# Softmax sums of queries 256 to 511 taken from exponentials of the first scores, on ScalarE instead of by matmul, in the last fifteen steps of an attention and mixture-of-experts layer

## The chip, the cores and the metric

One core of a Trainium2 chip runs the whole program in one launch. The metric is the device time in microseconds, here a median of three runs.

## The reference, cut to what matters

The layer adds three things: its input x (8 batches x 512 tokens x 512 features), causal attention over the layer norm of x (16 heads of 32), and a top-2-of-8 expert layer over the same norm.

```python
xn = _layernorm(x)
q, k, v = proj(Wq), proj(Wk), proj(Wv)          # 16 heads of 32
q, k = _apply_rope(q, k)
scores = einsum('bhqd,bhkd->bhqk', q, k) / sqrt(32)
scores = where(causal, scores, finfo.min)
attn = softmax(scores)
out = einsum('bhqk,bhkd->bhqd', attn, v) @ Wo.T
x = x + out + experts(xn)
```

The softmax needs, for each query and head, the largest score and the sum of the exponentials. The change concerns that sum.

## The kernel before, in words

The attention is cut into 32 steps n, one for each batch and each group of four heads (HG = 4). Steps 0 to 15 come first, then the experts (71 tiles, lines 801 and 1137), then steps 16 to 31. Every engine has its own program, written out by hand in a fixed order (`step(n)` in the blocks of TensorE, VectorE and ScalarE), and the engines meet at semaphores. No scheduler moves anything: an instruction that waits holds up all that stands behind it on its engine.

The scores are computed twice.

* **First scores** (`scores(m, k)`, line 886), queries on partitions, keys along the row. Their only use is the largest score of each query. Eleven score units k = 0 to 10 (`S_UNITS`, line 245) cover the four heads and the four query blocks i of 128. Units 0 to 2 hold the query blocks 0 and 1 of several heads. Units 3 to 6 are block 2 (384 keys) of heads 0 to 3, units 7 to 10 are block 3 (512 keys). They alternate between two PSUM banks (`BANK_S + k % 2`). VectorE reduces each to its maximum (`largest_score`, line 1322, the instruction on line 1326), and unit k + 2 may be written when unit k is reduced (line 893). Step n does this for step n + 1: it is the look-ahead of one step.
* **Shifted scores** (`shifted_scores(n, k)`, line 906), keys on partitions, queries along the row. The maxima were split into two f16 parts (`split_c`), turned by TensorE (`turn_c`, line 902), copied by ScalarE (`copy_c`, line 705) and sent through DRAM into two more rows of `q_stack`, so that the matmul itself subtracts them. Eleven shifted units go through two banks (`BANK_T`), and ScalarE's `exps(n, k)` (line 696, instruction on line 702) writes their exponentials to `pT`. GpSimd zeroes the masked triangle.

`times_v(n, j)` (line 919) then works on the key block j (0 to 3) of `pT`, queries j x 128 to 511. Four matmuls of 32 output rows, one for each head, add P times V into `BANK_O` (line 928). Four more with a matrix of ones (`ones32`, line 931) add the sums of the exponentials into `BANK_DEN`. All are f32 and run over 512, 384, 256 and 128 columns. Blocks 0 and 1 are done in step n, blocks 2 and 3 in step n + 1. VectorE's `normalise_o(n)` (line 1337) waits for the last of them, turns the sums, takes reciprocals and scales the output; ScalarE's `high_o` (line 711) rounds it for the output projection.

Between these, TensorE's program lays pieces of other work that wait for little: the projections of Q, K and V for later steps (lines 948, 957) and the output projection (line 966). A stretch of TensorE's step reads: shifted unit j, score unit j + 4, three projection matmuls, shifted unit j + 1, score unit j + 5, and so on. VectorE's step does score maxima 0 to 3, `normalise_o(n - 1)`, `rotate(0)` for Q (line 1313), maxima 4 to 8, `rotate(1)`, maxima 9 and 10, `split_c`. Steps 29 to 31 have no projections of Q and K left, steps 28 to 31 none of V, and steps 16 to 27 have all.

## Time and profile before

| | |
|---|---|
| median of three runs | 1181.91 us (1181.77 to 1182.01) |
| the profiled execution's own time | 1190.92 us |
| its span, first to last instruction | 1189.0 us |
| mean granted TensorE clock | 0.916 of full speed |
| TensorE matmuls busy | 984.2 us, 83% of the span |
| VectorE busy | 733.6 us, 62% |
| ScalarE busy | 416.3 us, 35% |
| GpSimd busy | 544.0 us, 46% |
| matmuls with the ones (line 931) | 1024, 94.0 us busy, mean 439 ns |
| P times V (line 928) | 1024, 100.1 us busy, mean 464 ns |
| exponentials (line 702) | 352, 224.1 us busy |
| score maxima (line 1326) | 352, 212.3 us busy |

Busy times count an engine's instructions from start to end, so where matmuls overlap in the array the sum over a group is more than what the group takes of the span. The profiled execution ran 9.0 us longer than the median of the three timed ones, and what the profile shows adds up to its span. Steps 16 to 31 begin at 826.6 us of the span. The program's last score unit stands at 1141.9 us.

### The profile page before, as it was taken

How to read it: one execution, taken by the hardware profiler on the slowest of the kernel's cores; microseconds unless marked ns; L12 is line 12 of the kernel's file. 1: busy time of each engine (PE TensorE's matmuls, PEld its weight loads, DVE VectorE, ACT ScalarE, POOL GpSimd, SP SyncE). 2: the span in 40 equal slices, each digit the busy share in tenths (PEclk: the TensorE clock that was granted, in tenths of full speed). 3: DMA queues.
4: the chain of work that ended last, by engine and by line, in shares of the span. 5: the costliest groups of instructions: out<-in, count | busy, mean ns of one | idle time of the engine just before them, and what ended most of it. 6: DMA issues, size and time to landing. Idle time of an engine off the chain costs nothing.

```text
span 1189.0 us, 18558 instructions
## 1 busy us (share of the span) xinstructions
PE 984.2 (83%) x6525; PEld 460.9 (39%) x6557; DVE 733.6 (62%) x1282; ACT 416.3 (35%) x689; POOL 544.0 (46%) x561
## 2 busy tenths in 40 slices
PE   3659675778769786987859999999999999999886
PEld 1224232333324332432435555554444444444332
DVE  7465665576557665785524444444777777777654
ACT  3243554354444333333311222211443443443441
POOL 1423543353443543457423333331766766765534
PEclk8888787898879887989979999999999999999899
DMA  5446164746655441243565555554546445435224
GB/s 201 120 145 218 44 235 112 229 133 204 205 204 183 155 159 55 73 145 114 205 219 174 175 176 171 177 177 153 179 160 195 147 162 196 143 126 182 83 73 141
DMA packets 107960, 188.60 MB, mean 159 GB/s; under 512 B 11872, under 2 KB 65248, under 8 KB 102624
## 3 DMA queue, kind: packets, MB, share of 16 engines
q1 hardware_dynamic: 97072, 152.03, 37.8%
q0 software_dynamic: 10800, 35.40, 10.2%
q8 instruction: 55, 0.90, 0.3%
q14 instruction: 33, 0.27, 0.1%
HBM read 117.13 MB, written 70.25 MB: 158 GB/s over the span
## 4 chain that ended last, share of the span: by engine, by line
PE 62%; DVE 15%; DMA 9%; issue 5%; ACT 4%; POOL 2%; SPq 2%; POOLq 0%; ACTq 0%; DVEq 0%
PE psum L880 16%; PE psum L948 8%; PE psum L957 7%; PE psum L928 6%; PE psum L897 6%; PE psum L966 5%; PE psum L931 5%; PE psum L915 4%; DVE top L1326 3%; DMA x_blk<-xn_rows 3%; PE psum L857 3%; DMA c_rows<-c_turn 3%; DVE rden L1341 2%; DVE den_turned L1339 2%; DVE turned_q L1319 1%
## 5 line engine op out<-in xcount | busy, mean ns | idle before, releaser
L702 ACT ACTIVATE pT<-psum,factors 128x512 f32<-128x512 f32 (+1 forms) x352 | 224.1, 642 | 466.4 <-PE psum L915 463.4
L897 PE MATMUL psum<-k_stack,q_stack 96*128 96x384 f16 (+3 forms) x512 | 140.4, 328 | 133.0 <-DVE top L1326 123.4
L1326 DVE TENSOR_REDUCE top<-psum 128x1 f32<-128x384 f32 (+3 forms) x352 | 212.3, 634 | 48.3 <-PE psum L899 36.3
L948 PE MATMUL psum<-xT,w_att 128*128 128x512 f16 x768 | 211.6, 404 | 9.4 <-DVE xT L1288 5.3
L880 PE MATMUL psum<-w_exp,x_gT 128*128 x852 | 197.9, 383 | 5.4 <-DVE x_gT L1293 5.4
L915 PE MATMUL psum<-q_stack,k_stack 98*128 98x256 f16 (+3 forms) x512 | 134.9, 316 | 7.1 <-ACT pT L702 6.2
L570 POOL DMA_INDIRECT x_g<-xn_rows,tok_of x71 | 67.3, 947 | 147.6 <-PE psum L857 146.4
L897 PEld LDWEIGHTS psum<-k_stack,q_stack 96*128 96x128 f16 x512 | 48.7, 102 | 198.5 <-DVE top L1326 157.0
L564 POOL TENSOR_TENSOR o_hl<-o_sb,o_hl 128x512 f16<-128x512 f32 x32 | 36.9, 1154 | 189.0 <-ACT o_hl L716 189.0
L558 POOL TENSOR_SCALAR_AFFINE_SELECT pT<-pT 128x512 f32<-128x512 f32 x128 | 86.9, 690 | 77.8 <-ACT pT L702 77.7
L880 PEld LDWEIGHTS psum<-w_exp,x_gT 128*128 128x128 f16 x852 | 83.8, 98 | 92.1 <-issue 8.5
L1307 DVE SCALAR_TENSOR_TENSOR y_sb<-psum,down,bias_all 128x512 f32<-128x512 f32 x71 | 53.3, 751 | 103.7 <-PE psum L880 103.7
L957 PE MATMUL psum<-w_att,xT 128*128 128x512 f16 x384 | 113.0, 426 | 0.0
L948 PEld LDWEIGHTS psum<-xT,w_att 128*128 128x128 f16 x768 | 73.7, 103 | 86.1 <-issue 22.9
L726 ACT ACTIVATE x_gT<-psum 128x512 f16<-128x512 f32 x71 | 42.4, 597 | 182.7 <-PE psum L857 182.7
L966 PE MATMUL psum<-w_att,o_hl 128*128 128x512 f16 x384 | 98.4, 383 | 4.5 <-POOL o_hl L564 4.5
L928 PE MATMUL psum<-pT,v_sb 128*32 128x512 f32 (+3 forms) x1024 | 100.1, 464 | 1.2 <-POOL pT L558 1.2
L931 PE MATMUL psum<-pT,ones 128*32 128x512 f32 (+3 forms) x1024 | 94.0, 439 | 0.0
L899 PE MATMUL psum<-causal,ident 128*128 128x128 bf16 (+1 forms) x320 | 79.2, 248 | 0.0
L915 PEld LDWEIGHTS psum<-q_stack,k_stack 98*128 98x128 f16 x512 | 46.1, 101 | 85.3 <-issue 42.6
L554 POOL TENSOR_TENSOR q_hl<-plain_q,q_hl 128x512 f16<-128x512 f32 x32 | 46.6, 1455 | 61.9 <-ACT q_hl L687 61.9
L580 POOL DMA_INDIRECT y_in<-y_rows,idx_y x64 | 62.6, 979 | 19.7 <-issue 11.1
(153 smaller groups left out, 1240.9 us busy)
## 6 DMA issues: line engine op xcount, KB each, us to landing
y_rows<-y_sb SPq DMA_DIRECT2D x71, 256.0 KB, 2.0
w_in<-w_all SPq DMA_DIRECT2D x12, 1024.0 KB, 8.9
q_stack<-qk_rows SPq DMA_DIRECT2D x96, 128.0 KB, 2.6
k_stack<-qk_rows SPq DMA_DIRECT2D x96, 128.0 KB
x_in<-x SPq DMA_DIRECT2D x8, 1024.0 KB, 9.1
xn_rows<-x_in SPq DMA_DIRECT2D x8, 1024.0 KB, 8.2
qk_rows<-q_hl SPq DMA_DIRECT2D x32, 256.0 KB, 2.1
qk_rows<-k_hl SPq DMA_DIRECT2D x32, 256.0 KB
```

The source lines that it names most:

```text
L558: pool.affine_select(out=p_diagonal(j), in_=p_diagonal(j), compare_op=ALU.is_ge, fill=0.0, base=0, pattern=[[0, HG], [1, P]], channel_mult ...
L702: act.activation(p_of(j, h, heads), banks[BANK_T + (NT_ * n + k) % 2][:, 0:W], ACT.Exp, scale=factors[:, 0:1]).then_inc(exp_done, 1)
L880: now = pe.matmul(banks[s % 4], x_gT[s % 4][:, xp * C + c, :], w_exp[:, bass.ds(e, 1), wp, c, :].rearrange("p e d -> p (e d)"), start=n == ...
L897: pe.matmul(bank[:, h * W:(h + 1) * W], q_stack[u][0:ROW_C, h0 + h, i * P:(i + 1) * P], k_stack[u][0:ROW_C, h0 + h, 0:W], start=h == 0, st ...
L899: pe.matmul(bank[:, 0:heads * W].rearrange("p (h t) -> p h t", h=heads)[:, :, W - P:W], ident16[:], causal[:, 0:heads, :], start=False, st ...
L915: now = pe.matmul(bank[:, h * W:(h + 1) * W], k_stack[u][0:ROW_C + 2, h0 + h, j * P:(j + 1) * P], q_stack[u][0:ROW_C + 2, h0 + h, j * P:S] ...
L928: pe.matmul(banks[BANK_O][h * HD:(h + 1) * HD, j * P:S], v_sb[b % 2][:, j, g * P + h * HD:g * P + (h + 1) * HD], p_of(j, h, 1), start=j == ...
L931: now = pe.matmul(banks[BANK_DEN][h * HD:(h + 1) * HD, j * P:S], ones32[:], p_of(j, h, 1), start=j == 0, stop=j == J - 1)
L948: now = pe.matmul(bank, w_att[:, what, wp, c, g * P:(g + 1) * P], xT[b % 2][:, xp * C + c, :], start=at_pass == 0, stop=at_pass == 3 * C - 1)
L957: now = pe.matmul(banks[bank], xT[b % 2][:, xp * C + c, j * P:(j + 1) * P], w_att[:, 2, wp, c, :], start=at_pass == 0, stop=at_pass == 3 * ...
L966: now = pe.matmul(banks[bank], o_hl[b % 2][:, c, xp, j * P:(j + 1) * P], w_att[:, 3, wp, c, :], start=at_pass == 0, stop=at_pass == 3 * C - 1)
L1326: return dve.tensor_reduce(out=top[:, h:h + heads, i], in_=banks[BANK_S + k % 2][:, 0:heads * W].rearrange("p (h t) -> p h t", h=heads), a ...
```

## The change

For steps n = 17 to 31 (`SUMS` = 17) the sums of query blocks 2 and 3 no longer come from `pT`. In the step before, after the maximum of score units 3 to 10, VectorE multiplies it by minus the scale (`shift_scores`, one number for each partition), and ScalarE takes the exponential of the unit's scores in place in PSUM, with that number as bias, and accumulates it along the row into `den` (`sum_scores`). `times_v` runs its matmuls with ones only over columns 0 to 255, thus for key blocks 0 and 1, and eight new matmuls of 128 columns bring `den` into columns 256 to 511 of `BANK_DEN`: `den`, broadcast over 32 columns, is the stationary operand and the f32 identity the moving one. TensorE's score units 5 to 10, and the next step's unit 0 and `turn_c`, now wait for ScalarE's `den_done`. The rest of the program is the same.

```diff
@@ ScalarE
+            def sum_scores(m, k):
+                h, _, i = S_UNITS[k]
+                here = banks[BANK_S + k % 2][:, 0:(i + 1) * P]
+                act.wait_ge(shift_done, sum_no(m, k))
+                act.activation(here, here, ACT.Exp, scale=factors[:, 1:2], bias=shift_s[:, h, i - J // 2:i - J // 2 + 1],
+                               accum_out=den[:, m % 2, h, i - J // 2:i - J // 2 + 1]).then_inc(den_done, 1)
...
             def step(n):
                 exps(n, 0)
+                if SUMS <= n + 1 < N:
+                    sum_scores(n + 1, 3)
                 exps(n, 1)
+                if SUMS <= n + 1 < N:
+                    sum_scores(n + 1, 4)
                 if n and n != N1:
                     high_o(n - 1)
...
                 exps(n, 2)
+                if SUMS <= n + 1 < N:
+                    sum_scores(n + 1, 5)
                 exps(n, 3)
+                if SUMS <= n + 1 < N:
+                    sum_scores(n + 1, 6)
                 exps(n, 4)
+                if SUMS <= n + 1 < N:
+                    sum_scores(n + 1, 7)
...
                 exps(n, 5)
+                if SUMS <= n + 1 < N:
+                    sum_scores(n + 1, 8)
...
                 exps(n, 6)
+                if SUMS <= n + 1 < N:
+                    sum_scores(n + 1, 9)
                 exps(n, 7)
+                if SUMS <= n + 1 < N:
+                    sum_scores(n + 1, 10)
                 if n + 1 < N:
                     copy_c(n + 1)
@@ TensorE
-                if k >= 2:
+                if k >= 2 and m >= SUMS and k - 2 in SUM_UNITS:
+                    pe.wait_ge(den_done, sum_no(m, k - 2))
+                elif k >= 2:
                     pe.wait_ge(max_done, NS * m + k - 1)
                 elif m:
                     pe.wait_ge(c_copied, m)
+                    if m > SUMS:
+                        pe.wait_ge(den_done, sum_no(m, 0) + SUM_UNITS[0] - 1)
...
             def turn_c(m):
                 pe.wait_ge(c_made, m + 1)
+                if m >= SUMS:
+                    pe.wait_ge(den_done, sum_no(m, NS - 2))
...
-                for h in range(HG):
-                    now = pe.matmul(banks[BANK_DEN][h * HD:(h + 1) * HD, j * P:S], ones32[:], p_of(j, h, 1),
-                                    start=j == 0, stop=j == J - 1)
+
+                upto = S if n < SUMS else S // 2
+                if j * P < upto:
+                    for h in range(HG):
+                        now = pe.matmul(banks[BANK_DEN][h * HD:(h + 1) * HD, j * P:upto], ones32[:], p_of(j, h, 1)[:, 0:upto - j * P],
+                                        start=j == 0, stop=(j + 1) * P == upto)
+                if n >= SUMS and j == 0:
+                    pe.wait_ge(den_done, sum_no(n, NS - 1))
+                    for i in range(J // 2):
+                        for h in range(HG):
+                            now = pe.matmul(banks[BANK_DEN][h * HD:(h + 1) * HD, (J // 2 + i) * P:(J // 2 + i + 1) * P],
+                                            den[:, n % 2, h, i:i + 1].broadcast_to([P, HD]), ident32[:], start=False, stop=False)
                 now.then_inc(pv_done, 1)
@@ VectorE
+                if m >= SUMS and k in SUM_UNITS:
+                    shift_scores(m, k)
+
+
+            def shift_scores(m, k):
+                h, _, i = S_UNITS[k]
+                dve.wait_ge(max_done, NS * m + k + 1)
+                dve.tensor_tensor(shift_s[:, h, i - J // 2:i - J // 2 + 1], top[:, h, i:i + 1], factors[:, 3:4], ALU.mult).then_inc(shift_done, 1)
```

Once, ahead of step 0, two more operations on one number for each partition make the scale and its negative (`factors[:, 1]` and `[:, 3]`).

**ScalarE**, from the rounding of K in one step to the exponentials of the next, one of steps 17 to 28. The names say what is written from what; `pT` are exponentials of shifted units, `o_hl` is `high_o`. Before:

```order
L687 ACTIVATE k_hl<-plain_k 128x512 [waits k_stored,qk_roped]
L702 ACTIVATE pT<-psum,factors 128x512 [waits pv_done,t_done] x4
L716 ACTIVATE o_hl_131<-o_sb 128x512 [waits o_read]
L702 ACTIVATE pT<-psum,factors 128x512 [waits pv_done,t_done] x2
L702 ACTIVATE pT<-psum,factors 128x384 [waits pv_done,t_done]
```

and with the change:

```order
L697 ACTIVATE k_hl<-plain_k 128x512 [waits k_stored,qk_roped]
L712 ACTIVATE pT<-psum,factors 128x512 [waits pv_done,t_done] x3
L719 ACTIVATE psum,den<-psum,shift_s,factors 128x384 [waits shift_done]
L712 ACTIVATE pT<-psum,factors 128x512 [waits pv_done,t_done]
L719 ACTIVATE psum,den<-psum,shift_s,factors 128x384 [waits shift_done]
L733 ACTIVATE o_hl_133<-o_sb 128x512 [waits o_read]
L712 ACTIVATE pT<-psum,factors 128x512 [waits pv_done,t_done]
L719 ACTIVATE psum,den<-psum,shift_s,factors 128x384 [waits shift_done]
L712 ACTIVATE pT<-psum,factors 128x512 [waits pv_done,t_done]
L719 ACTIVATE psum,den<-psum,shift_s,factors 128x384 [waits shift_done]
```

A sum stands behind each exponential of the shifted units 0 to 4 (and behind those of 5 to 7), and `high_o` now has two of them ahead of it.

**TensorE**, the same place in the step, from shifted unit 1 to the projection matmuls behind score unit 6. Before:

```order
L915 MATMUL psum<-q_stack_96,k_stack_99 128x512 [waits exp_done]
L897 MATMUL psum<-k_stack_100,q_stack_97 128x384 [waits max_done]
L899 MATMUL psum<-causal,ident_49 128x128
L948 MATMUL psum<-xT_133,w_att 128x512 [waits sum_done]
L948 MATMUL psum<-xT_133,w_att 128x512 x2
L915 MATMUL psum<-q_stack_96,k_stack_99 128x512 [waits exp_done]
L897 MATMUL psum<-k_stack_100,q_stack_97 128x384 [waits max_done]
L899 MATMUL psum<-causal,ident_49 128x128
L948 MATMUL psum<-xT_133,w_att 128x512 x3
```

and with the change:

```order
L954 MATMUL psum<-q_stack_97,k_stack_100 128x512 [waits exp_done]
L934 MATMUL psum<-k_stack_101,q_stack_98 128x384 [waits den_done]
L936 MATMUL psum<-causal,ident_49 128x128
L996 MATMUL psum<-xT_135,w_att 128x512 [waits sum_done]
L996 MATMUL psum<-xT_135,w_att 128x512 x2
L954 MATMUL psum<-q_stack_97,k_stack_100 128x512 [waits exp_done]
L934 MATMUL psum<-k_stack_101,q_stack_98 128x384 [waits den_done]
L936 MATMUL psum<-causal,ident_49 128x128
L996 MATMUL psum<-xT_135,w_att 128x512 x3
```

No instruction moved, but each score unit from unit 5 on (line 934, before 897) waits for ScalarE's sum of the unit two before it instead of VectorE's maximum.

**VectorE**, from the end of `rotate(0)` to `rotate(1)` and, in the first fence, the two maxima behind it. Before:

```order
L1320 TENSOR_TENSOR plain_q<-psum,trig_sb 128x512
L1326 TENSOR_REDUCE top<-psum 128x1 [waits s_done] x5
L1319 STREAM_SHUFFLE turned_k<-psum 128x512 [waits qk_lo,qk_summed]
L1320 TENSOR_TENSOR plain_k<-psum,trig_sb 128x512
L1326 TENSOR_REDUCE top<-psum 128x1 [waits s_done] x2
```

and with the change:

```order
L1368 TENSOR_TENSOR plain_q<-psum,trig_sb 128x512
L1374 TENSOR_REDUCE top<-psum 128x1 [waits s_done]
L1383 TENSOR_TENSOR shift_s<-top,factors 128x1 [waits max_done]
L1374 TENSOR_REDUCE top<-psum 128x1 [waits s_done]
L1383 TENSOR_TENSOR shift_s<-top,factors 128x1 [waits max_done]
L1374 TENSOR_REDUCE top<-psum 128x1 [waits s_done]
L1383 TENSOR_TENSOR shift_s<-top,factors 128x1 [waits max_done]
L1374 TENSOR_REDUCE top<-psum 128x1 [waits s_done]
L1383 TENSOR_TENSOR shift_s<-top,factors 128x1 [waits max_done]
L1374 TENSOR_REDUCE top<-psum 128x1 [waits s_done]
L1383 TENSOR_TENSOR shift_s<-top,factors 128x1 [waits max_done]
L1367 STREAM_SHUFFLE turned_k<-psum 128x512 [waits qk_lo,qk_summed]
```

Behind every maximum of a unit of one head there is one more instruction, which waits for the maximum just written.

## Rows read from the trace of the kernel before

**Rows 1.** The page: busy time of each engine; TensorE's granted clock, in 40 slices of 29.7 us

```profile
PE 984.2 (83%) x6525; PEld 460.9 (39%) x6557; DVE 733.6 (62%) x1282; ACT 416.3 (35%) x689; POOL 544.0 (46%) x561
...
PEclk8888787898879887989979999999999999999899
```

**Rows 2.** Busy us (count) of PE, PEld, DVE, ACT, POOL; granted clock, DMA share, GB/s

```profile
826.00:1110.00 284.00, 267.81 (x1949) 123.75 (x1963) 213.06 (x358) 116.19 (x205) 195.69 (x215) 1.00 0.49 163
```

**Rows 3.** Chain that ended last, one step: the four sums by matmul (start, us, what)

```profile
929.46 0.86 PE psum L931 x8
...
935.33 0.65 PE psum L931 x8
...
940.14 0.43 PE psum L931 x8
...
940.79 0.26 PE psum L931 x8
```

**Rows 4.** TensorE in order of time, step 21: start, us, engine, line, [idle before]

```profile
940.94 0.39 PE L915 MATMUL psum<-q_stack,k_stack 98*128 98x512 f16 x1
...
943.77 0.38 PE L915 MATMUL psum<-q_stack,k_stack 98*128 98x512 f16 x1
945.29 0.34 PE L897 MATMUL psum<-k_stack,q_stack 96*128 96x384 f16 x1 [1.14 <-DVE top L1326]
...
946.39 0.38 PE L897 MATMUL psum<-k_stack,q_stack 96*128 96x512 f16 x1
...
949.66 0.38 PE L897 MATMUL psum<-k_stack,q_stack 96*128 96x512 f16 x1
```

**Rows 5.** VectorE in order of time, the same step

```profile
939.38 1.16 DVE L1326 TENSOR_REDUCE top<-psum 128x2 f32<-128x512 f32 x2 [0.45 <-PE psum L899]
941.07 0.72 DVE L1339 STREAM_TRANSPOSE den_turned<-psum 128x512 f32<-128x512 f32 x1 [0.54 <-PE psum L931]
...
944.69 1.59 DVE L1326 TENSOR_REDUCE top<-psum 128x1 f32<-128x384 f32 x3
```

**Rows 6.** Groups by line and form on ScalarE, whole span: count, busy us, mean ns

```profile
L702 ACT ACTIVATE pT<-psum,factors 128x512 f32<-128x512 f32 x224 | 150.5, 678 | 310.5 <-PE psum L915 308.0
L702 ACT ACTIVATE pT<-psum,factors 128x384 f32<-128x384 f32 x128 | 73.8, 578 | 156.0 <-PE psum L915 155.4
...
L649 ACT ACTIVATE x_in<-x_in,shift,rstd 128x512 f32<-128x512 f32 x32 | 23.9, 801 | 0.0
...
L644 ACT ACTIVATE std<-var_eps 128x4 f32<-128x4 f32 x8 | 1.6, 202 | 8.9 <-DVE var_eps L1166 8.9
```

**Rows 7.** ScalarE in order of time, two exponentials' neighbours in that step

```profile
943.10 0.69 ACT L702 ACTIVATE pT<-psum,factors 128x512 f32<-128x512 f32 x1 [1.05 <-PE psum L915]
943.69 0.62 ACT L716 ACTIVATE o_hl<-o_sb 128x512 f16<-128x512 f32 x1
```

**Rows 8.** Groups by line and form on VectorE: an operation on one number per partition

```profile
L1190 DVE TENSOR_SCALAR expo<-amax_all 128x1 f32<-128x1 f32 x13 | 2.0, 154 | 0.4
```

**Rows 9.** TensorE in order of time, steps 29 and 30

```profile
1116.48 0.39 PE L915 MATMUL psum<-q_stack,k_stack 98*128 98x512 f16 x1
...
1119.61 0.50 PE L897 MATMUL psum<-k_stack,q_stack 96*128 96x384 f16 x1 [1.57 <-DVE top L1326]
...
1123.00 0.63 PE L897 MATMUL psum<-k_stack,q_stack 96*128 96x512 f16 x1
...
1136.00 0.39 PE L915 MATMUL psum<-q_stack,k_stack 98*128 98x512 f16 x1
...
1141.89 0.63 PE L897 MATMUL psum<-k_stack,q_stack 96*128 96x512 f16 x1
```

**Rows 10.** Busy time by stretch, a part of step 29, columns as in rows 2

```profile
1119.60:1126.40 6.80, 6.79 (x30) 2.35 (x30) 5.50 (x10) 3.15 (x6) 1.79 (x2) 0.51 0.01 3
```

**Rows 11.** TensorE in order of time, step 1

```profile
126.08 0.63 PE L897 MATMUL psum<-k_stack,q_stack 96*128 96x512 f16 x1
...
128.28 0.61 PE L897 MATMUL psum<-k_stack,q_stack 96*128 96x512 f16 x1
```

More of the change, by code:

```diff
@@ L53, in moe_attention_layer @@
     EARLY = N1 - G
+    SUMS = N1 + 1
     x_v = x.rearrange("b (j p) d -> b p j d", p=P)
@@ L99, in moe_attention_layer @@
     down = at("down", [P, 16], I32)
-    factors = at("factors", [P, 3], F32)
+    factors = at("factors", [P, 4], F32)
     gate_hl = at("gate_hl", [P, C, 2 * E], F16)
@@ L121, in moe_attention_layer @@
     top = at("top", [P, HG, J], F32)
+    shift_s = at("shift_s", [P, HG, J // 2], F32)
+    den = at("den", [P, 2, HG, J // 2], F32)
     c_hl = at("c_hl", [P, 2, HG * J], F16)
@@ L251, in moe_attention_layer, with sum_no @@
     ROW_C = 3 * HD
+    SUM_UNITS = [k for k in range(NS) if S_UNITS[k][2] >= J // 2]
+    def sum_no(m, k):
+        return len(SUM_UNITS) * (m - SUMS) + k - SUM_UNITS[0] + 1
     NORM_AT = {0: 2, 2: 3, 3: 4, 5: 5, 6: 6, 8: 7}
@@ L927, in times_v @@
                 for h in range(HG):
-                    pe.matmul(banks[BANK_O][h * HD:(h + 1) * HD, j * P:S], v_sb[b % 2][:, j, g * P + h * HD:g * P + (h + 1) * HD],
+                    now = pe.matmul(banks[BANK_O][h * HD:(h + 1) * HD, j * P:S], v_sb[b % 2][:, j, g * P + h * HD:g * P + (h + 1) * HD],
                               p_of(j, h, 1), start=j == 0, stop=j == J - 1)
-                for h in range(HG):
-                    now = pe.matmul(banks[BANK_DEN][h * HD:(h + 1) * HD, j * P:S], ones32[:], p_of(j, h, 1),
-                                    start=j == 0, stop=j == J - 1)
+                upto = S if n < SUMS else S // 2
[9 more added lines that the diff above has]
+                                            den[:, n % 2, h, i:i + 1].broadcast_to([P, HD]), ident32[:], start=False, stop=False)
                 now.then_inc(pv_done, 1)
@@ L1325, in largest_score @@
                 dve.wait_ge(s_done, NS * m + k + 1)
-                return dve.tensor_reduce(out=top[:, h:h + heads, i], in_=banks[BANK_S + k % 2][:, 0:heads * W].rearrange("p (h t) -> p h t", h=heads),
-                                         axis=AX.X, op=ALU.max).then_inc(max_done, 1)
+                dve.tensor_reduce(out=top[:, h:h + heads, i], in_=banks[BANK_S + k % 2][:, 0:heads * W].rearrange("p (h t) -> p h t", h=heads),
+                                  axis=AX.X, op=ALU.max).then_inc(max_done, 1)
+                if m >= SUMS and k in SUM_UNITS:
[4 more added lines that the diff above has]
+                dve.tensor_tensor(shift_s[:, h, i - J // 2:i - J // 2 + 1], top[:, h, i:i + 1], factors[:, 3:4], ALU.mult).then_inc(shift_done, 1)
             def split_c(m):
@@ L1472, in _ @@
             own.link(dve.tensor_tensor(factors[:, 0:1], q_, k_, ALU.mult))
-            dve.tensor_scalar(factors[:, 0:1], factors[:, 0:1], 2.0 ** (2 * LOG_QK) * HD ** -0.5, None, ALU.mult).then_inc(qk_factor, 1)
+            own.link(dve.tensor_scalar(factors[:, 0:1], factors[:, 0:1], 2.0 ** (2 * LOG_QK) * HD ** -0.5, None, ALU.mult))
+            own.link(dve.tensor_scalar(factors[:, 1:2], factors[:, 0:1], 2.0 ** -90, None, ALU.max))
+            dve.tensor_scalar(factors[:, 3:4], factors[:, 1:2], -1.0, None, ALU.mult).then_inc(qk_factor, 1)
             dve.wait_ge(gate_in, 16)
```

1 line of the change is left out of this document (added).

## The prediction

> **What bounds the kernel now.** I read first the page's busy times and the granted clock in slices [rows 1]: TensorE is at 83% of the span, ScalarE at 35%, so the change moves work from the full engine to the emptiest one. But shares of the span are averages. In steps 16 to 28 matmuls fill 267.8 of 284 us at clock 1.00 [rows 2], so a matmul taken out there is time gained, unless TensorE then waits for something else. The chain that ended last gives what the sums by matmul take of the path in one step: 0.86, 0.65, 0.43 and 0.26 us [rows 3]. TensorE's timeline of that step shows its one large wait, 1.14 us in front of score unit 6, for the maximum of unit 4 [rows 4]. VectorE's timeline says why that maximum is late: it stands behind `normalise_o` and `rotate(0)`, which start only when the last sums are in, at 941.07, and it starts at 944.69 [rows 5]. That is the stretch into which the change puts ScalarE.
>
> I count the step from shifted unit 0 at 940.94 (T below). Before: score unit 6 starts at T+4.35, unit 7 at T+5.45, and with 1.09 us from unit to unit, unit 10 at T+8.72 [rows 4]. Only unit 6 waits.
>
> **What the change removes from TensorE.** Four heads run side by side in the array, so columns give the price: 512 are 0.86, 256 are 0.43, 128 are 0.26 [rows 3]. Block 0 has 256 columns left and twice four new matmuls of 128: 0.43 + 2 x 0.26 = 0.95 instead of 0.86. Block 1 falls from 0.65 to 0.26, blocks 2 and 3 go (0.43, 0.26). Together 1.0 us less a step, 15 steps: **-15 us**. I assume that the new matmuls, with a broadcast as stationary operand, run four at a time as those with the ones do. If they ran one after another, eight at 0.21 each (a quarter of 0.86 is the time of 128 columns in four turns) would be 1.7 instead of 0.5: 18 us more over 15 steps.
>
> **What it adds on VectorE.** After each maximum an operation on one number, 0.15 us [rows 8], and it waits for the maximum to be written, some 0.04: 0.19 us, eight times a step. The one after maximum 3 also holds up `normalise_o`: blocks 2 and 3 of the sums are gone and TensorE reaches T 0.7 earlier after score unit 3, but the maximum and its product take what they took, so the normalisation starts at about T+0.5 instead of T+0.13 [rows 5]. Maximum 4 then starts at T+4.1 instead of T+3.75, ends at T+4.65, and the product is there at T+4.85.
>
> **What it adds on ScalarE.** No row has an accumulated row sum or a write to PSUM. From below, an exponential of 512 is 0.68 and of 384 is 0.58 with one operand from memory (the scale); an activation of 512 with two (shift and scale) is 0.80 [rows 6]. Neighbours start 0.59 after one another where one takes 0.69 [rows 7], so 0.1 overlaps. A sum of 512 thus holds the engine 0.70 us and one of 384 some 0.60, without the accumulator. Reading it out costs nothing at best, and at worst as much as the smallest instruction there, 0.20 [rows 6], or a little more. I take 0.15, between the two and nearer the instruction: 0.85 and 0.75. The Trainium skill (ScalarE: Activation LUTs, What happens when an `exp` ACTIVATE runs) says that ScalarE writes PSUM faster than SBUF. It gives no figure, and no row here has such a write; 0.05 less on each sum would take some 4 us off the result.
>
> **The walk.** ScalarE runs in order, and TensorE's score unit k + 2 now waits for sum k. Sum 4 runs from T+4.85 to T+5.7, so unit 6 starts at **T+5.8**, 1.45 later than before. ScalarE then has `high_o` (0.53), exponential 2 (0.59) and sum 5 (0.75) before unit 7 may start: T+7.7. Exponential 3 and sum 6 (1.34): unit 8 at T+9.05. Exponential 4 and sum 7 (0.50 + 0.85): unit 9 at T+10.4. `high_qk(0)` (0.52), exponential 5 and sum 8 (0.50 + 0.85): unit 10 at **T+12.3**, against T+8.72. Each pair has 1.09 us of work on TensorE and 1.3 to 1.9 on ScalarE: here ScalarE, 35% busy over the span, is the bound. After unit 10 TensorE has P times V, projections and output projections, and sums 9 and 10 fall beside these, so nothing more is lost, and `copy_c`, late by some 3 us, still has the rest of the step for its way through DRAM. Loss: 3.6 us a step in steps 16 to 28, **+46.8**, less 1 because step 16 normalises nothing.
>
> Steps 29 and 30 have no projections as filler. From T to unit 10 they take 6.5 and 5.9 us now [rows 9]. ScalarE's walk there has no `high_qk` and starts about 1.2 earlier, as VectorE has no `rotate(0)`, and gives T+10.3: **+8.2** for both. Sum without the clock: 46.8 - 1 + 8.2 - 15 = +39.
>
> **The clock.** In steps 29 and 30 a wait of 1.57 us in front of unit 6, with small ones ahead of it, ended with matmuls at the low level [rows 9]: the granted clock was 0.51 from 1119.6 to 1126.4, thus 1.2 instead of 2.4 GHz [rows 10]. Waits of 1.14 in steps 17 to 28 did not do that [rows 2, 4]. With the change the wait in front of unit 6 goes from T+3.0 to T+5.8, 2.8 us, and others of 0.3 to 0.8 follow. So I expect low stretches in most steps. At 1.2 GHz a pair took 2.20 us [rows 11]. Where ScalarE gives 1.3 to 1.9, part of it is hidden. At worst all four pairs from unit 6 to 10 take 2.20, 8.8 instead of 6.5: 2.3 a step, 35 in all. At best nothing. A stretch of half that length, in most steps, costs about 0.8 a step: **+12**.
>
> Sum: 39 + 12 = 51 us. The profiled execution took 1190.9 us (span 1189.0), 9 above the median; the same 51 go on either. 1181.9 + 51 gives **1233 us**.
>
> **Rivals.**
>
> 1. **ScalarE keeps up (faster).** It is idle 65% of the span, and the loss at unit 6 hangs on one latency. For the change to win, the delay from unit 6 to unit 10 must stay under 1.0 us a step. Fully hidden it would give 1181.9 - 15 = 1167 us. Against it: the same walk with sums as short as a plain exponential's spacing (0.49 for 384, 0.59 for 512) still has unit 6 late by 1.1 and unit 10 by 2.1. Only a maximum 4 that came earlier would help, and VectorE's order is kept. Chance 0.05.
> 2. **The clock stays up.** Waits of 1.14 left it at 1.00 [rows 2, 4], and between units 6 and 10 TensorE still works three quarters of the time. Then 39 are left: 1221 us. Chance 0.25.
> 3. **The clock falls in every step and stays down until unit 10.** 39 + 35 = 74: 1256 us. The Trainium skill (TensorE: Matmul & The Clock Gate, A second HAM failure mode: psum-queue depth-cycling) says that a TensorE which idles briefly and often between groups, while it cycles through PSUM banks, makes the clock oscillate. By that rule every step would fall. The trace agrees for steps 29 and 30 and not for steps 17 to 28, where the same two banks alternate and the clock stayed at 1.00 [rows 2, 10]. Chance 0.15.
> 4. **The new matmuls do not run side by side**, so that the change does not take off TensorE what it says: 18 more, 1251 us. Chance 0.05.
>
> The forecast, with low stretches in most steps, has 0.48. The last 0.02 is for gain and loss cancelling out.
>
> **How the numbers follow.** The low end is the walk with a free accumulator and no clock loss: five sums of the walk at 0.15 less are 0.75 a step, 11 us, so 1210, and a few less with cheap writes to PSUM: 1204. The high end takes the accumulator at 0.25 (five times 0.10, 7.5 us) and nearly the whole clock loss: 1181.9 + 39 + 7.5 + 30 = 1258. A measurement of this kernel can tell 0.2%, 2.4 us, from no change. Faster has rival 1 alone, 0.05; within 0.2% is 0.02; slower is the rest, 0.93.
>
> **What would show it.** Right: TensorE's wait in front of score unit 6 at 2.5 us or more, now ended by ScalarE, with smaller ones in front of units 7 to 10; the steps 17 to 28 each 2.6 to 3.4 us longer; ScalarE with hardly a gap from sum 4 to sum 8; sums of 512 at 0.8 to 1.0 us; matmuls with ones and `den` down by about 1.0 us a step on the chain; granted clock under 1.00 in the slices past 826. Wrong: score unit 6 still ended by VectorE's maximum; a sum of well over 1 us or of two instructions (then the walk holds but is too short); a clock of 1.00 throughout; a wait in front of `turn_c`, the next step's unit 0 or its shifted unit 0, since I cost sums 9 and 10 and the late `copy_c` at nothing, behind the projections that lie there.

## The result, and the profile after

The changed kernel takes **1238.1 us** (median of four runs, 1231.1 to 1242.1) against 1182.0 us: a ratio of **1.046 [1.040, 1.051]**, slower by 56 us. The profiled execution took 1238.7 us with a span of 1236.8, against 1190.9 and 1189.0. So the two traces lie 47.8 us apart, and it is these 47.8 that can be followed row by row.

The page of the changed kernel: busy times, the granted clock in 40 slices, and the chain that ended last by engine.

```profile
PE 987.9 (80%) x6525; PEld 461.3 (37%) x6557; DVE 770.8 (62%) x1404; ACT 500.3 (40%) x929; POOL 541.5 (44%) x561
...
PEclk9889787888889888999799999999899999999888
...
PE 55%; DVE 17%; DMA 10%; ACT 8%; issue 7%; POOL 2%; SPq 2%; POOLq 0%; ACTq 0%; DVEq 0%
```

The stretch of [rows 2] in the changed kernel (columns as there):

```profile
826.00:1110.00 284.00, 245.27 (x1726) 111.45 (x1737) 212.16 (x397) 161.10 (x351) 168.98 (x189) 0.95 0.46 146
```

ScalarE gained 84 us of work over the span and stands at 40%, the emptiest engine still. But TensorE's matmuls fill only 245.3 of 284 us where they filled 267.8, and the granted clock is 0.95 where it was 1.00. The waits of steps 16 to 31 (826 to 1237) say on whom TensorE now waits. Engine and line, released by, us in total, times, longest:

```profile
PE psum L934 <- ACT psum L719: 53.0, 55, 3.0
...
ACT psum L719 <- DVE shift_s L1383: 35.6, 26, 2.6
```

53 us of waits in front of score units (line 934), all ended by ScalarE's sums (line 719). ScalarE in turn waits for VectorE's product (line 1383).

TensorE in order of time in step 21, the step of [rows 4]. Shifted unit 0 starts at 962.47, which is T here; the five score units below are 6 to 10.

```profile
962.47 0.39 PE L954 MATMUL psum<-q_stack,k_stack 98*128 98x512 f16 x1
...
968.02 0.34 PE L934 MATMUL psum<-k_stack,q_stack 96*128 96x384 f16 x1 [2.34 <-ACT psum L719]
...
969.77 0.39 PE L934 MATMUL psum<-k_stack,q_stack 96*128 96x512 f16 x1 [0.49 <-ACT psum L719]
...
971.00 0.39 PE L934 MATMUL psum<-k_stack,q_stack 96*128 96x512 f16 x1
...
972.46 0.39 PE L934 MATMUL psum<-k_stack,q_stack 96*128 96x512 f16 x1 [0.20 <-ACT psum L719]
...
974.23 0.39 PE L934 MATMUL psum<-k_stack,q_stack 96*128 96x512 f16 x1 [0.51 <-ACT psum L719]
```

Unit 6 starts at T+5.55 and unit 10 at T+11.76, where they started at T+4.35 and T+8.72: 3.04 us are lost between T and unit 10. ScalarE over the same stretch, from exponential 0 to sum 7:

```profile
962.89 0.69 ACT L712 ACTIVATE pT<-psum,factors 128x512 f32<-128x512 f32 x1 [5.02 <-PE psum L954]
963.48 0.64 ACT L719 ACTIVATE psum<-psum,shift_s,factors 128x384 f32<-128x384 f32 x1
964.03 0.20 ACT L719 ACTIVATION_READ_ACCUMULATOR psum<-psum,shift_s,factors 128x1 f32 x1
964.63 0.69 ACT L712 ACTIVATE pT<-psum,factors 128x512 f32<-128x512 f32 x1 [0.40 <-PE psum L954]
967.20 0.64 ACT L719 ACTIVATE psum<-psum,shift_s,factors 128x384 f32<-128x384 f32 x1 [1.88 <-DVE shift_s L1383]
967.77 0.19 ACT L719 ACTIVATION_READ_ACCUMULATOR psum<-psum,shift_s,factors 128x1 f32 x1
967.86 0.62 ACT L733 ACTIVATE o_hl<-o_sb 128x512 f16<-128x512 f32 x1
968.38 0.68 ACT L712 ACTIVATE pT<-psum,factors 128x512 f32<-128x512 f32 x1
968.95 0.64 ACT L719 ACTIVATE psum<-psum,shift_s,factors 128x384 f32<-128x384 f32 x1
...
971.54 0.74 ACT L719 ACTIVATE psum<-psum,shift_s,factors 128x512 f32<-128x512 f32 x1
972.20 0.20 ACT L719 ACTIVATION_READ_ACCUMULATOR psum<-psum,shift_s,factors 128x1 f32 x1
```

The first wait, 1.88 us, is for the product of maximum 4. Behind it there is hardly a gap up to sum 8. An accumulated sum is **two instructions**. The second reads the accumulator, takes 0.20 us and starts while the first is still running: from sum 4 at 967.20 to `high_o` at 967.86 are 0.66 us, and a sum of 512 holds the engine 0.75 to 0.78 (971.54 to 972.32, where `high_qk` follows). Unit 6 starts 0.06 behind the end of the accumulator read at 967.96, and units 7 to 10 start 0.05 to 0.06 behind theirs.

VectorE in that step: the start of `normalise_o`, maximum 4, its product, and the product of maximum 6:

```profile
962.82 0.71 DVE L1395 STREAM_TRANSPOSE den_turned<-psum 128x512 f32<-128x512 f32 x1
...
966.43 0.54 DVE L1374 TENSOR_REDUCE top<-psum 128x1 f32<-128x384 f32 x1
967.01 0.16 DVE L1383 TENSOR_TENSOR shift_s<-top,factors 128x1 f32<-128x1 f32 x1
...
969.04 0.69 DVE L1383 TENSOR_TENSOR shift_s<-top,factors 128x1 f32<-128x1 f32 x1
```

Groups by line and form, 840 to 1200 us, on ScalarE and VectorE (count, busy us, mean ns, idle before):

```profile
L719 ACT ACTIVATE psum<-psum,shift_s,factors 128x512 f32<-128x512 f32 x60 | 44.8, 747 | 8.8 <-DVE shift_s L1383 8.7
L719 ACT ACTIVATE psum<-psum,shift_s,factors 128x384 f32<-128x384 f32 x59 | 37.9, 643 | 26.9 <-DVE shift_s L1383 26.9
...
L719 ACT ACTIVATION_READ_ACCUMULATOR psum<-psum,shift_s,factors 128x1 f32 x119 | 23.8, 200 | 0.0
```
```profile
L1383 DVE TENSOR_TENSOR shift_s<-top,factors 128x1 f32<-128x1 f32 x119 | 51.6, 434 | 4.1
```

What TensorE was to save it does save. In order of time, P times V and the sums of key block 0 in step 20, the new matmuls (line 979) behind them:

```profile
951.88 0.61 PE L973 MATMUL psum<-pT,ones 128*32 128x256 f32 x8
952.31 0.62 PE L979 MATMUL psum<-ident,den 128*32 128x128 f32 x16
952.86 0.34 PE L954 MATMUL psum<-q_stack,k_stack 98*128 98x384 f16 x1
```

The eight new matmuls (each shows twice, as all f32 ones here do) take 0.55 us (952.31 to 952.86), so they run side by side. Block 1 in step 20, and P times V of blocks 2 and 3 ahead of T of step 21:

```profile
957.75 0.40 PE L973 MATMUL psum<-pT,ones 128*32 128x128 f32 x8
958.08 0.61 PE L1014 MATMUL psum<-w_att,o_hl 128*128 128x512 f16 x2
...
961.67 0.86 PE L967 MATMUL psum<-pT,v_sb 128*32 128x256 f32 x16
```

From start to start, block 0 takes 0.98 us as before (929.28 to 930.25 there, 0.97), block 1 0.33 instead of 0.76 (935.15 to 935.91), and from P times V of blocks 2 and 3 to T it is 0.80 instead of 1.44 (939.50 to 940.94). Together 1.06 us a step.

**Where the 47.8 us are.** From T to T, steps 17 to 27 took 22.27 us each before. Now they take 24.27 where the clock stays up and 25.26 where a low stretch falls into them, one with the clock at 1.2 instead of 2.4 GHz, which is in seven of the eleven (the first of them 25.84). The one of step 19, in the columns of [rows 2], with a clock of 0.56:

```profile
919.80:923.20 3.40, 3.40 (x11) 1.33 (x10) 2.82 (x6) 2.36 (x6) 2.44 (x3) 0.56 0.00 0
```

The sum of a step: 24.27 is 22.27 + 3.04 - 1.06, within 0.02. From T of step 17 to T of step 31 it is 337.4 us for 299.7: **+37.7**, of which steps 28 to 30 have 8.2. Step 16 has +5.4, and **+4.6** had been lost before step 16 began: its first score unit starts at 831.2 instead of 826.6, and the same shows already at the normalisation of step 15 (597.8 for 592.9), in code that the change leaves alone. The tail adds 0.2.

### The profile page after: what moved, and what is told of

Same layout as the page of the kernel before. It is cut to its first block, busy times and chain, and to the rows that moved or that the text cites. A ratio compares the mean times of both kernels' runs of the same rounds, so it can differ in the third digit from the quotient of the medians.

```text
span 1236.8 us, 18963 instructions
## 1 busy us (share of the span) xinstructions
PE 987.9 (80%) x6525; PEld 461.3 (37%) x6557; DVE 770.8 (62%) x1404; ACT 500.3 (40%) x929; POOL 541.5 (44%) x561
## 4 chain that ended last, share of the span: by engine, by line
PE 55%; DVE 17%; DMA 10%; ACT 8%; issue 7%; POOL 2%; SPq 2%; POOLq 0%; ACTq 0%; DVEq 0%
PE psum L913 15%; PE psum L996 7%; PE psum L1005 7%; PE psum L967 5%; PE psum L1014 5%; PE psum L934 5%; DVE top L1374 4%; PE psum L954 4%; DMA x_blk<-xn_rows 3%; PE psum L973 3%; PE psum L890 3%; DMA c_rows<-c_turn 3%; ACT psum L719 2%; ACT pT L712 2%; DVE rden L1397 1%
## 5 line engine op out<-in xcount | busy, mean ns | idle before, releaser
L996 PE MATMUL psum<-xT,w_att 128*128 128x512 f16 x768 | 216.2, 411 | 9.2 <-DVE xT L1336 5.1
L719 ACT ACTIVATE psum<-psum,shift_s,factors 128x384 f32<-128x384 f32 (+1 forms) x120 | 83.4, 695 | 35.7 <-DVE shift_s L1383 35.6
L590 POOL DMA_INDIRECT y_in<-y_rows,idx_y x64 | 62.7, 980 | 19.7 <-issue 11.1
```

The source lines that it names most:

```text
L719: act.activation(here, here, ACT.Exp, scale=factors[:, 1:2], bias=shift_s[:, h, i - J // 2:i - J // 2 + 1], accum_out=den[:, m % 2, h, i - ...
L996: now = pe.matmul(bank, w_att[:, what, wp, c, g * P:(g + 1) * P], xT[b % 2][:, xp * C + c, :], start=at_pass == 0, stop=at_pass == 3 * C - 1)
```

## The experiments

Twelve kernels ran on three further chips, four on each. Ratios are to the kernel before on the same chip, with 95% intervals; on these chips its median was 1205.3, 1206.7 and 1201.7 us. In the diffs - is the changed kernel, unless the text names another.

**1. The sums on ScalarE, and TensorE keeps its own** (`adds_only`).

```diff
-                upto = S if n < SUMS else S // 2
...
+                for h in range(HG):
+                    now = pe.matmul(banks[BANK_DEN][h * HD:(h + 1) * HD, j * P:S], ones32[:], p_of(j, h, 1),
+                                    start=j == 0, stop=j == J - 1)
```

> Only what the change adds: shifts, sums and their waits as in the changed kernel, but the matmuls with ones run over all columns as before, and the eight matmuls with den are left out (den is not read). Theory (ScalarE's chain between score units 6 and 10 makes the loss, and the removed matmuls give back 1.0 us a step): 15 steps x 1.0 slower than the changed kernel, 1253 us, with a step of 25.3 us where the clock stays up. Rival (the new matmuls with a broadcast stationary operand, or their wait, are a part of the loss): near 1238 or below. Rival (ScalarE had slack and TensorE's own work set the end): the whole 15 us show as well, but the wait in front of unit 6 gets shorter by as much as TensorE comes later.

Measured: 1273.7 us, 1.057 [1.050, 1.064]. The change itself is at 1.042 and 1.046 (experiment 6 and the first chip), so TensorE's part gives back 1.1 to 1.5%, 13 to 18 us, beside the sums on ScalarE. The whole loss, and more, comes with the sums. The comparison is one between chips, and no step from 17 on keeps its clock up here (27.4 to 28.4 us in steps 17 to 27), so the 1.0 us a step can't be read from single steps.

**2. TensorE's part alone** (`removes_only`): the sums, the products and the waits for them are gone.

```diff
-                if SUMS <= n + 1 < N:
+                if False:
                     sum_scores(n + 1, 3)
...
-                if m >= SUMS and k in SUM_UNITS:
+                if False:
                     shift_scores(m, k)
```

> Only what the change takes from and gives to TensorE: fewer matmuls with ones, the eight matmuls with den (which holds a constant, so the sums of queries 256 to 511 in the last fifteen steps are left out), no shifts, no sums, no waits for ScalarE. Theory: 1.0 us less in each of 15 steps, 1182 - 15 = 1167 us, a step of 21.3 us instead of 22.27, and the wait in front of unit 6 as before, 1.1 us. Rival (the wait in front of unit 6 grows by what TensorE saves, since VectorE then sets the pace): 1175 to 1182 us.

Measured: 1207.8 us, 1.002 [0.999, 1.005]. The order of the two is as expected: adding costs, removing doesn't. But the gain of 1.3% that the removal should have brought isn't there, though TensorE does the smaller work. The stretch 850 to 1120 says why in part, here for this kernel:

```profile
850.00:1120.00 270.00, 242.54 (x1774) 114.89 (x1772) 188.37 (x318) 102.44 (x179) 171.42 (x188) 0.94 0.48 152
```

and for the kernel before on one of these chips (experiment 5):

```profile
850.00:1120.00 270.00, 240.10 (x1733) 110.19 (x1734) 188.15 (x318) 102.48 (x181) 172.01 (x188) 0.98 0.45 148
```

Clock 0.94 against 0.98, in low stretches in eight of the steps 17 to 27 against two. These traces are of two chips, but runs on one chip say the same: over the whole span the granted clock of this kernel was 0.905 to 0.913 in ten runs, that of the kernel before beside it 0.916 to 0.929. The clock is not all of it. In these two traces the first score unit of step 16 starts at 827.7 instead of 821.5, and nothing ahead of it was changed (the early loss, below). One of the steps 17 to 27 of `removes_only` has neither a low stretch nor the lateness told in experiment 5. It took 21.23 us, 1.04 less than the 22.27 of the kernel before on the first chip: the removal's price again. The others took 22.2 to 25.9.

**3. The sums without the accumulator** (`no_accumulator`).

```diff
-                act.activation(here, here, ACT.Exp, scale=factors[:, 1:2], bias=shift_s[:, h, i - J // 2:i - J // 2 + 1],
-                               accum_out=den[:, m % 2, h, i - J // 2:i - J // 2 + 1]).then_inc(den_done, 1)
+                act.activation(here, here, ACT.Exp, scale=factors[:, 1:2], bias=shift_s[:, h, i - J // 2:i - J // 2 + 1]).then_inc(den_done, 1)
```

> The changed kernel with the same exponentials in place but without accumulation into den (which holds a constant: the sums of queries 256 to 511 in the last fifteen steps are left out). The trace shows reading the accumulator as an instruction of its own of 0.20 us, of which 0.10 delays the next. Theory (ScalarE paces units 6 to 10, five sums in the walk): 0.5 us less a step, 7 us in all, 1231 us. Rival (VectorE's shifts, some of which take over 1 us, pace the units): no change, 1238 us.

Measured: 1250.7 us, 1.035 [1.029, 1.042], thus 0.7 to 1.1% (8 to 13 us) less than the change on two other chips. The intervals touch, so the size is rough; the rows show the place. ScalarE in order of time, sum 4 and `high_o`:

```profile
970.77 0.64 ACT L719 ACTIVATE psum<-psum,shift_s,factors 128x384 f32<-128x384 f32 x1 [2.52 <-DVE shift_s L1382]
971.34 0.62 ACT L732 ACTIVATE o_hl<-o_sb 128x512 f16<-128x512 f32 x1
```

The next instruction starts 0.57 behind the sum, where it was 0.66. So reading the accumulator out holds the engine some 0.1 us of its 0.20. Unit 6, which waits for the end of the sum, starts 0.70 behind its start (971.47) instead of 0.82: also 0.1 sooner, not 0.2.

**4. The wait in front of unit 6 filled with matmuls** whose result nobody reads (`filled_wait`).

```diff
                 if nxt:
+                    if N1 <= n < N - 1:
+                        pe.wait_ge(o_read, n)
+                        for _ in range(8):
+                            pe.matmul(banks[BANK_DEN], ident16[:], w_att[:, 0, 0, 0, :], start=True, stop=True)
                     scores(n + 1, 6)
```

> The changed kernel with eight matmuls of 512 columns into the free bank BANK_DEN in TensorE's wait in front of score unit 6, 1.73 us of the 2.34 us wait, in steps 16 to 30. Theory (steps of 25.26 instead of 24.27 us are those in which the granted clock fell): clock 1.00 in steps 17 to 28 and all of these steps at 24.27 us, 7 x 1.0 less there and a few us less in steps 29 and 30: 1228 us. Rival (something else, as DMA or GpSimd, makes every other step longer): the clock stays up, steps still alternate, 1238 us. Rival (the fill itself delays unit 6): steps of over 24.5 us throughout.

Measured: 1241.7 us, 1.028 [1.022, 1.035]. TensorE in order of time: the fill, and score unit 6 behind it,

```profile
966.71 1.90 PE L1072 MATMUL psum<-w_att,ident 128*128 128x512 f16 x8
969.38 0.34 PE L934 MATMUL psum<-k_stack,q_stack 96*128 96x384 f16 x1 [0.78 <-ACT psum L719]
```

and the stretch 850 to 1120:

```profile
850.00:1120.00 270.00, 240.84 (x1756) 108.37 (x1754) 198.83 (x379) 152.04 (x334) 160.46 (x180) 1.00 0.46 146
```

The clock is at 1.00 and none of the steps 17 to 27 has a low stretch. Step 26, the only one of them without the lateness told in experiment 5, takes the 24.27 us that were expected of all, the others 25.1 to 25.8. The kernel, which does more work, is 1.4 to 1.7% faster than the unfilled one (1.042 in experiment 6, 1.046 on the first chip): 17 to 21 us. So a good third of the change's loss hangs on the clock on these chips. The waits for ScalarE remain, and with them the rest.

**5 and 6. Both kernels unchanged** on one of these chips.

> The kernel before, unchanged, to have its trace on the chip of the other runs of this job. The only-removing kernel gave 1.0016 of the time before where 0.987 was expected, with VectorE's normalisation and ScalarE's first exponential starting some 1.6 us late in most of the last fifteen steps, which the first trace of the kernel before does not show. Theory (that lateness belongs to the chip and not to the kernel): where it shows in the other traces of this job it shows here too, and the ratio is 1.000. Rival (it comes from the changed matmuls): no such lateness here.

> The changed kernel, unchanged, as the reference for this job. Ratio 1.046 as on the first chip, within 0.01. Steps 17 to 28 in two lengths 1.0 us apart, the longer ones with a stretch of low clock.

Measured: 1207.3 us, 1.000 [0.998, 1.003], and 1258.6 us, 1.042 [1.039, 1.046]. The ratio is that of the first chip, but both kernels are slower in absolute time, by 20 to 25 us. In the changed kernel every one of the steps 17 to 27 has a low stretch here, and they take 25.25 to 27.43 us, not the two lengths expected. Where the kernel before loses its time, the waits of 850 to 1120 show:

```profile
PE psum L897 <- DVE top L1326: 30.0, 12, 2.7
...
DVE den_turned L1339 <- remote: 16.3, 8, 2.1
```

The normalisation starts 1.64 us behind T instead of 0.13, though nothing of this core that the trace shows is late, and so does exponential 0; maximum 4 and unit 6 follow (wait 2.64 instead of 1.14), and a step takes 23.75 us instead of 22.27. Steps up to 16 and from 28 on don't show it. The wait of 1.14 in [rows 4] is thus not a property of the kernel alone. Here before has 2.6 us in front of unit 6 in each step and nearly always keeps its clock, while `removes_only` with 2.1 to 2.9 loses it. The length of that one wait doesn't decide the clock. What the edit changes is that TensorE has fewer matmuls around it; that this is the cause is argued, not shown by a run of its own.

**7 and 8. Maxima 4 and 5 ahead of `rotate(0)`**, in the kernel before and in the changed one.

```diff
+                if n >= N1 and nxt:
+                    largest_score(n + 1, 4)
+                    largest_score(n + 1, 5)
                 if ahead:
                     rotate(0, n + 3)
...
-                if nxt:
+                if nxt and n < N1:
                     largest_score(n + 1, 4)
                     largest_score(n + 1, 5)
```

> The kernel before, with VectorE's score maxima 4 and 5 ahead of rotate(0) in steps 16 to 30. Theory (the one wait of TensorE in these steps, 1.14 us in front of unit 6, hangs on maximum 4 standing behind normalise_o and rotate(0)): 1.0 to 1.1 us less in each of steps 17 to 28, 12 to 13 us in all, a ratio of 0.989. Rival (rotate(0), now later, delays Q and what follows by as much): ratio 1.00.

> The changed kernel, with VectorE's score maxima 4 and 5 ahead of rotate(0) in steps 16 to 30. Theory (ScalarE's chain from sum 4 to sum 8 begins with maximum 4, so all of it moves by the 1.3 us of rotate(0)): unit 6 at 4.3 us after shifted unit 0 instead of 5.55, a step 1.2 us shorter, some 15 us in all and a few more by the clock: ratio to before 1.030 or less. Rival (the number of ScalarE's instructions and not where they begin sets the step): 1.040 or more.

Measured: before with it 1197.9 us, **0.993 [0.991, 0.995]**, the only kernel of this study that beats both; the changed kernel with it 1228.7 us, 1.018 [1.014, 1.023], 2.4% less than without. TensorE's waits in front of the scores fall from the 30.0 us of experiment 5 to

```profile
PE psum L897 <- DVE top L1326: 15.2, 9, 1.8
```

In this trace of the kernel before, four of the steps 17 to 27 have a low stretch (two in experiment 5), which takes back a part: with the clock up its steps take 22.5 us on average instead of 23.8. In the changed kernel steps 17 to 27 take 23.9 us in most cases, and the clock stays up in nine of eleven, where experiment 6 has a low stretch in all. So a part of the 2.4% is the clock's. With the clock up in both, the nine steps take 23.9 us on average against 25.4 in experiment 4, and that is the order's own. The chain of the change begins at maximum 4, then: start it earlier and what follows on ScalarE moves with it.

**9 and 10. `removes_only` again, and with the fill of experiment 4**, on the third chip.

> The kernel that only removes, once more, beside the next one. On a chip on which the normalisation starts 1.6 us late (the kernel before at 1206 us) the theory is now that low clock eats the gain: ratio 1.00 and a low stretch in most steps. On a chip without the lateness (the kernel before at 1182 us, the wait in front of unit 6 at 1.1 us) the first expectation stands: ratio 0.987, clock up.

> The kernel that only removes, with eight matmuls of 512 columns into the free bank BANK_DEN in TensorE's wait in front of score unit 6 (steps 16 to 30). Theory (the removal is worth 1.0 us a step and was eaten by low clock that the larger share of idle time brought): clock at 1.00 in steps 17 to 28, and 12 to 15 us below the kernel before, ratio 0.987 to 0.990. Rival (the wait in front of unit 6 grows by what TensorE saves, whatever the clock): ratio 1.00 with the clock up as well.

Measured: 1212.2 us, 1.009 [1.006, 1.013] (the same kernel was at 1.002 in experiment 2, so the clock's loss differs with the chip), and 1199.6 us, 0.998 [0.995, 1.001]. The stretch 850 to 1120, unfilled:

```profile
850.00:1120.00 270.00, 239.40 (x1718) 112.80 (x1727) 182.59 (x308) 100.11 (x176) 169.81 (x186) 0.92 0.46 146
```

and filled:

```profile
850.00:1120.00 270.00, 257.19 (x1905) 123.34 (x1916) 192.00 (x324) 104.27 (x183) 178.29 (x196) 0.99 0.49 156
```

Clock 0.92 and 0.99, and 12.7 us between the medians: this much of the time of `removes_only` hung on the clock. But the filled kernel falls short of its expectation, and a ratio of 1.00 with the clock up is what the rival named. The steps speak against that rival: the nine of 17 to 27 without a low stretch take 22.8 us on average, those of the kernel before in experiment 5 (on another chip) 23.8, so nearly all of the removal's 1.0 us is there. What takes it back lies elsewhere. The first score unit of step 16 starts at 830.5 instead of 821.5 (the early loss, below), and the fill has to wait until `normalise_o` is through with its banks, a new wait on TensorE (9.1 us in eight waits between 850 and 1120). How much of the 1.3% would be left without these wasn't measured.

**11. `high_qk(0)` behind sum 8** (`round_q_late`).

```diff
-                if n + 3 < N:
+                if n + 3 < N and n < N1:
                     high_qk(0, n + 3)
                 exps(n, 5)
                 if SUMS <= n + 1 < N:
                     sum_scores(n + 1, 8)
+                if n + 3 < N and n >= N1:
+                    high_qk(0, n + 3)
```

> The changed kernel, with ScalarE's rounding of Q (high_qk(0), 0.52 us of its time) behind sum 8 instead of ahead of exponential 5, in steps 16 to 28. Theory (everything on ScalarE between sums 4 and 8 delays unit 10 by its length): 0.5 us a step, 6 to 7 us in all, ratio to before 1.037 to 1.040. Rival (ScalarE has gaps there, waiting for VectorE's shifts or TensorE's units, that take it up): no change, 1.042 to 1.046.

Measured: 1255.5 us, 1.044 [1.042, 1.047]; the change itself was at 1.042 and 1.046 on two other chips, so no gain can be told. Every one of the steps 16 to 30 has a low stretch, 102.8 us of them from T of step 16 on, for 90.3 in experiment 6. There ScalarE waits for TensorE's shifted units, as the rival has it. In step 20 it has a wait of its own in front of exponential 5, where the rounding stood:

```profile
956.16 0.58 ACT L712 ACTIVATE pT<-psum,factors 128x384 f32<-128x384 f32 x1 [0.64 <-PE psum L956]
```

Step 26, the one without the lateness in both traces and with one low stretch in each, takes 24.73 us for 25.25, the 0.5 less of the expectation. So with the clock up the rounding may well cost its length; that wasn't tested.

**12. Only query block 3 on ScalarE** (units 7 to 10), with maxima 4 and 5 first and `high_qk(0)` late (`last_block`).

```diff
-    SUM_UNITS = [k for k in range(NS) if S_UNITS[k][2] >= J // 2]
+    SUM_UNITS = [k for k in range(NS) if S_UNITS[k][2] >= J - 1]
```

> A version that may beat both: sums on ScalarE for queries 384 to 511 alone (score units 7 to 10), so only units 9 and 10 wait for it, with maxima 4 and 5 ahead of rotate(0) and the rounding of Q behind sum 8. It takes 0.6 us of matmuls off a step instead of 1.0. Theory (ScalarE's chain, now of two sums, still ends after unit 10's old place by 0.9 us): about 0.3 us a step more than maxima_first_before, ratio to before 0.995 to 1.000. Rival (the few sums fit into ScalarE's gaps): ratio 0.985, below maxima_first_before's 0.993.

Measured: 1219.2 us, 1.015 [1.013, 1.018]. Unit 6 waits for VectorE again (1.83), and the steps take 24.0 us with the clock up, no less than the 23.9 with all eight sums on ScalarE (experiment 8). This was a miss: half the sums do not remove the loss. Against experiment 7, step 20 of each, unit 6 starts at T+5.8 instead of T+5.1, as the normalisation starts 2.8 us behind T instead of 2.1 (the lateness of experiment 5); unit 9 waits another 0.52 us for ScalarE's sum, and unit 10 is at T+11.1 instead of T+9.5.

**The early loss.** VectorE's wait for loads of `x_blk` between 60 and 600 us, ahead of every line that the change touches, in the kernel before, and in the changed one:

```profile
DVE x_blk L1283 <- DMA x_blk<-xn_rows: 20.5, 6, 5.7
```
```profile
DVE x_blk L1331 <- DMA x_blk<-xn_rows: 27.9, 6, 7.1
```

It is 20.1 and 19.1 us in the two other traces of the code before, and 24.4 to 28.4 in all eleven of kernels built from the changed code, on every chip. The first score unit of step 16 starts at 819.2 to 826.6 in the three traces of the code before (822.4 on average) and at 826.9 to 831.2 in the eleven (829.7). So the loss goes with the changed program, not with the chip, and at 7 us on average it may be larger than the 4.6 of the first two traces: the trace before of the first chip, at 826.6, is the latest of its three, and it ran 9 us above its median. Why the same loads land later is open; no kernel was made for it.

## Why the prediction was right

The forecast was 1233 us in a range of 1204 to 1258, slower with a chance of 0.93. It came out at 1238.1, by the mechanism foreseen. By its steps:

* **What bounds the kernel.** Right: a mean share of 35% said nothing of the stretch from maximum 4 to unit 10. Experiments 7 and 8 show that this chain starts at maximum 4. In steps 17 to 27 TensorE has no wait over 0.25 us but those in front of units 6 to 10, so sums 9 and 10 and the late `copy_c` were rightly put at nothing.
* **Removal, 1.0 us a step.** Measured 1.06 on the first chip and 1.04 in `removes_only`. The new matmuls run side by side, so rival 4 is out. The figure is one at full clock: experiments 2 and 9 show that, taken alone, the removal pays nothing over the whole kernel, because the clock falls and the early loss comes on top.
* **VectorE's products, 0.19 us each.** Right where it counts: 0.16, and maximum 4's is there at T+4.70 (forecast T+4.85), the normalisation at T+0.35 (T+0.5). The mean of 0.43 us is a surprise, told below.
* **ScalarE's sums, 0.75 and 0.85 us.** Each 0.1 too long: 0.65 and 0.75. The accumulator's read does cost the 0.2 of the smallest instruction, as the text bounded it from above, but half of it lies beside the exponential. The walk also gave sum 4, one of 384, the price of a 512 (0.85). A sum of two instructions was to be a sign that the walk is too short; the two came, and the walk was too long. Put into the walk, the shorter sums and the earlier product of maximum 4 give unit 10 at T+11.76 for T+12.3 and a loss of **3.04 instead of 3.6** us a step. On writes to PSUM, which the Trainium skill ("ScalarE: Activation LUTs", Step-by-step: what each stage is for) calls faster than writes to SBUF, the rows agree in direction: 0.747 us for 512 elements from and to PSUM with two operands from memory, where the nearest row before had 0.801 from and to SBUF [rows 6]. Which side of it is cheaper no run tells apart.
* **The wait in front of unit 6.** Forecast "2.5 us or more", found 2.34, so narrowly wrong: the product and the sum came earlier by 0.15 and 0.1, and TensorE reached the wait at T+3.2 instead of T+3.0. The waits in front of 7, 9 and 10 (0.49, 0.20, 0.51) are as described; unit 8 has none.
* **The clock, +0.8 a step.** Right in kind and size: low stretches in seven of eleven steps at 1.0 us each are 0.6 a step. "Low stretches in most steps" holds on the first chip; in experiment 6 all eleven have one. Rival 2 (clock up, 1221 us) and rival 3 (all steps, 1256 us) lie to either side. The rule that rival 3 took from the Trainium skill ("TensorE: Matmul & The Clock Gate", A second HAM failure mode: psum-queue depth-cycling), that a TensorE which idles briefly and often makes the clock oscillate, fits experiments 4 and 10, where fewer and shorter pauses keep it up. It doesn't by itself say which of two kernels with such pauses falls: before paused 2.6 us a step in experiment 5 and mostly kept its clock.
* **Steps of 2.6 to 3.4 us more.** Found 2.0 without and 3.0 with a low stretch; the lower one is outside, above all by the 0.1 too much in each of five sums.
* **Missed.** Step 16 cost 5.4 where the text gave it 2.6 and a share of the clock. And 4.6 us go before step 16, in code that the change doesn't touch; no step of the working could have held them. What remains adds up. Twelve steps at 3.04 are 36.5, the removal in 14 steps is -14.8, seven low stretches are 7.0, steps 17 and 28 lost 0.6 and 1.0 more than their neighbours, and steps 29 and 30 lost 7.4 for the 8.2 of the text: 37.7 in all, the figure of the trace. That the result ended only 5 us above the forecast is in part two errors against each other: sums costed too dear, and the early loss not seen. Between the two traces it is 47.8, 3 below the 51 of the sum.

The median of the runs is 8 us further from the median before than the two profiled executions are from each other. The before profile was itself 9 us above its median, and the trace after lies within 1 us of its own (runs of 1231 to 1242).

## What to carry to other kernels

An engine that is idle two thirds of the span can still be the bound of the one stretch in which all waits end in turn; before work is moved to it, walk through that stretch instruction by instruction with the durations of the rows. Taking matmuls off TensorE where it already pauses may lower the granted clock (0.909 over the span for 0.924 here, medians on one chip) and so give back what it gains. So look at the clock row first, and close the pauses first. Here that was to be had by two maxima put ahead of a rotation, 0.7% for a change of order.

## What the runs showed of the hardware

**One number per partition can take 1.9 us on VectorE.** The products took 0.158 us at least, 0.159 in the middle, and up to 1.88; over the 119 of 840 to 1200 us the excess is 51.6 - 119 x 0.159 = 33 us. Of the 46 over 0.2 us, 45 end within 0.02 us of a GpSimd TENSOR_TENSOR that started first. The longest, 1.88 us from 838.50, is the exception: the GpSimd instruction with which it ends started 0.58 behind it. The product of maximum 6 runs from 969.04 to 969.73, and GpSimd in order of time has

```profile
968.56 1.16 POOL L574 TENSOR_TENSOR o_hl<-o_sb,o_hl 128x512 f16<-128x512 f32 x1 [4.26 <-ACT o_hl L733]
```

which ends at 969.72. In the same way a product of 1.17 us from 974.26 ends at 975.43 with a GpSimd instruction that ends at 975.41. The Trainium skill ("SBUF — State Buffer", Who interferes with whom) says that a VectorE instruction with two inputs in SBUF shares its second read interface with GpSimd, and that whichever starts first keeps it to its end. The rows agree, but for that one. The maxima, which read PSUM, are not held: maximum 6 took 0.56 from 968.45, beside the same instruction. In step 21 the delay of maximum 6's product costs nothing, as sum 6 stands behind exponential 3 (970.17), and that of maximum 9's holds up sum 9 by 0.82 us, behind unit 10. An operation with one input in SBUF and a constant was not tried in its place.

**Reading ScalarE's accumulator** is an instruction of its own of 0.20 us, half of which overlaps the activation (experiment 3).

**A lateness of 1.1 to 2.9 us behind T**, 1.6 in the kernel before, came and went with the chip (experiment 5), in steps 17 to 27 alone. On the first chip neither kernel has it, on the other three all twelve traces have it in most of these steps. What it is stays open.
